# The maxima of a unit are carried by three copies of 16 rows instead of one of 48

## The reference, cut to what matters

```
x = x + 0.5 * ffn(layernorm(x))     # ffn: x and weight rounded to an MXFP4-like grid, in blocks of 32
x = x + attn(layernorm(x))          # 16 heads of 8 features, rotary positions, full softmax over 512 keys
x = x + 0.5 * ffn(layernorm(x))

scores = einsum('bhqd,bhkd->bhqk', q, k) / sqrt(8)
out    = einsum('bhqk,bhkd->bhqd', softmax(scores), v)
```

## Time and profile before

| | |
|---|---|
| median of three runs | 591.27 us |
| profiled execution | 590.53 us |
| its span, first to last instruction | 588.5 us |
| TensorE matmul busy | 487.7 us (83%) |
| VectorE busy | 438.6 us (75%) |
| ScalarE busy | 398.7 us (68%) |
| GpSimd busy | 230.9 us (39%) |
| mean granted TensorE clock | 0.947 |

### The profile page before, as it was taken

One profiled execution on the slowest core, in us unless ns is written; L12 is line 12 of the kernel. 1 busy time (PEld: TensorE's weight loads), 2 busy tenths in 40 slices (PEclk: granted clock), 3 DMA queues, 4 the chain that ended last, 5 costly groups with the idle time before them and its releaser, 6 DMA issues.

```text
span 588.5 us, 10108 instructions
## 1 busy us (share of the span) xinstructions
PE 487.7 (83%) x2662; PEld 171.2 (29%) x2662; DVE 438.6 (75%) x1020; ACT 398.7 (68%) x766; POOL 230.9 (39%) x350
## 2 busy tenths in 40 slices
PE   1261879899899998999889888999899997998861
PEld 0121223332233333333223233333233322322211
DVE  6346979785989689967968597867996686889215
ACT  4816158686868787778748685778777774778740
POOL 4401173326544455446432544346442713012300
PEclk9996599999999999999979999999999997999995
DMA  3305304500350027001600034001600161000000
GB/s 83 94 9 138 67 11 109 100 2 11 99 109 20 3 57 159 8 17 46 161 14 20 11 99 109 15 5 51 161 6 19 33 155 31 20 1 2 19 1 18
DMA packets 22590, 30.81 MB, mean 52 GB/s; under 512 B 4998, under 2 KB 20236, under 8 KB 20236
## 3 DMA queue, kind: packets, MB, share of 16 engines
q1 hardware_dynamic: 20908, 29.87, 21.0%
q10 hardware_dynamic: 1632, 0.39, 0.3%
HBM read 21.47 MB, written 8.39 MB: 51 GB/s over the span
## 4 chain that ended last, share of the span: by engine, by line
PE 52%; issue 11%; DVE 10%; DMA 9%; POOL 9%; ACT 5%; SPq 2%; POOLq 1%; DVEq 0%; ACTq 0%
PE ot L1104 15%; PE sc L1091 13%; PE st L1080 11%; DMA feat_q<-maxrows 8%; DVE negmax L878 4%; POOL qkpre L457 3%; PE misc L1027 2%; PE misc L1069 2%; ACT probs L632 2%; PE misc L1044 2%; PE misc L1052 1%; ACT feat_k L522 1%; DVE stats_f L746 1%; DMA feat_k<-parts_k 1%; PE misc L1061 1%
## 5 line engine op out<-in xcount | busy, mean ns | idle before, releaser
L878 DVE TENSOR_REDUCE negmax<-sc 128x1 f32<-128x512 f32 x512 | 333.0, 682 | 88.7 <-PE sc L1091 88.2
L632 ACT ACTIVATE probs<-st 128x512 f32<-128x512 f32 x512 | 272.4, 599 | 89.0 <-PE st L1080 87.9
L1091 PE MATMUL sc<-feat_k,feat_q 96*128 96x512 bf16 x512 | 190.4, 397 | 10.2 <-DVE negmax L878 9.1
L1080 PE MATMUL st<-feat_q,feat_k 99*128 99x512 bf16 x512 | 157.1, 384 | 16.9 <-DMA feat_q<-maxrows 10.6
L1104 PE MATMUL ot<-probs,vfeat 128*32 128x512 f32 x1024 | 139.6, 618 | 1.0 <-ACT probs L632 1.0
L1091 PEld LDWEIGHTS sc<-feat_k,feat_q 96*128 96x128 bf16 x512 | 49.9, 98 | 167.3 <-DVE negmax L878 117.0
L1080 PEld LDWEIGHTS st<-feat_q,feat_k 99*128 99x128 bf16 x512 | 49.6, 99 | 87.6 <-ACT probs L632 43.8
L457 POOL TENSOR_TENSOR qkpre<-qkpre,ropeT 128x512 f32<-128x512 f32 x28 | 35.6, 1271 | 45.7 <-ACT qkpre L581 45.7
L442 POOL TENSOR_SCALAR maxparts<-negmax 128x16 bf16<-128x16 f32 x32 | 8.2, 257 | 90.6 <-DVE negmax L878 90.6
L1044 PE MATMUL misc<-xnT,wqkT 128*128 128x512 f32 x56 | 30.8, 633 | 2.7 <-DVE onorm L895 2.0
L481 POOL TENSOR_TENSOR xres<-xres,onorm 128x128 f32 (+1 forms) x31 | 14.1, 453 | 46.9 <-DVE onorm L895 46.9
(11 more groups left out here) (132 smaller groups left out, 471.6 us busy)
## 6 DMA issues: line engine op xcount, KB each, us to landing
feat_q<-parts_q SPq DMA_DIRECT2D x48, 192.0 KB
feat_k<-parts_k SPq DMA_DIRECT2D x48, 192.0 KB
parts_q<-qkparts_q SPq DMA_DIRECT2D x24, 128.0 KB, 2.3
parts_k<-qkparts_k SPq DMA_DIRECT2D x24, 128.0 KB, 2.3
xres<-in_L_attn_x_dram SPq DMA_DIRECT2D x8, 256.0 KB, 4.8
out_dram<-xres SPq DMA_DIRECT2D x8, 256.0 KB, 2.3
feat_q<-maxrows ACTq DMA_DIRECT2D x32, 12.0 KB
wload<-in_L_ffn_weight_dram SPq DMA_DIRECT2D x1, 64.0 KB, 2.4
```

The source lines that it names most:

```text
L632: nc.scalar.activation(probs[:, s % US, j * S:(j + 1) * S], st[:, bank(2 * s + j), :], ACT.Exp, scale=SCALE).then_inc(exp_done, 1)
L878: nc.vector.tensor_reduce(negmax[:, g, j:j + 1], sc[:, bank(16 * g + j), :], AX.X, ALU.max, negate=True).then_inc(sc_maxed, 1)
L1080: nc.tensor.matmul(st[:, bank(2 * s + j), :], feat["k"][par][0:MROWS, h, kb * P:(kb + 1) * P], feat["q"][par][0:MROWS, h, :], start=True, ...
L1091: nc.tensor.matmul(sc[:, bank(16 * g + j), :], feat["q"][par][0:SROWS, h, t * P:(t + 1) * P], feat["k"][par][0:SROWS, h, :], start=True, s ...
```

## The change

`load_max_rows` issues three DMAs, one for each part, in place of one. Each carries the 16 rows of a part from 16 partitions of `maxrows` to one partition of `feat_q`. The bytes and their places are the same. Each of the three adds 16 to the semaphore, so the two waits on it count in steps of 48 (`ROWS`).

```diff
+        ROWS = PARTS * 16
...
                 if after(2 * b + g // 2):
-                    act.wait_ge(max_loaded[g % 2], 16 * (2 * b + g // 2))
+                    act.wait_ge(max_loaded[g % 2], ROWS * (2 * b + g // 2))
...
                 act.wait_ge(max_rows, G * b + g + 1)
-                act.dma_start(feat["q"][par][SROWS:SROWS + PARTS, UH * g:UH * (g + 1), :]
-                              .rearrange("a h (t q) -> a (h t) q", q=P), maxrows[:, g % 2, :]).then_inc(max_loaded[g % 2], 16)
+                n = UH * T
+                for a in range(PARTS):
+                    act.dma_start(feat["q"][par][SROWS + a:SROWS + a + 1, UH * g:UH * (g + 1), :]
+                                  .rearrange("o h (t q) -> o (h t) q", q=P),
+                                  maxrows[n * a:n * (a + 1), g % 2, :]).then_inc(max_loaded[g % 2], 16)
...
                 if s % US == 0 and j == 0:
-                    pe.wait_ge(max_loaded[g % 2], 16 * (2 * b + g // 2) + 16)
+                    pe.wait_ge(max_loaded[g % 2], ROWS * (2 * b + g // 2) + ROWS)
```

## The result

The changed kernel takes 607.52 us (median of four runs, 602.08 to 617.5) beside 590.87 us: the ratio is 1.027, with an interval of 1.019 to 1.034. It is slower, by 16.7 us of the medians. The forecast was 601 us, 10.4 us more than the kernel before, with a range of 585 to 613 us. The sign and the range hold. The forecast's own narrower range, 594 to 605 us, does not, and "the same within 2%" had been given the larger chance (0.54 against 0.36 for slower). That the time lies inside the wide range is in part luck: one term was far too small, and another came out at nothing.

The account below looks back on a forecast made before the run. TensorE, busy 487.7 of 588.5 us, was taken as the bound. Landings 7.9, spread -1.2, ScalarE's issues 1.0 and clock 2.7 gave 10.4 us on 590.53 us: 601 us, range 585 to 613 us.

Parts of the forecast that it names:

- Landing late behind the loads: Units of g = 2: the third copy stands behind loads SyncE issued meanwhile; 7.9 us, less 1.2 us for the spread.
- the seven crowded units: Units g = 2, one per batch from first to seventh, whose copies are issued while SyncE loads the next batch's features.
- The term of 7.9 - 1.2 us: Crowded g = 2 units: 7.9 us for later third copies, less 0.3 us off four landings for rows spread over more engines.
- the stall is absorbed by the wait: Units of g = 2: exponentials come 1 us late, but TensorE then waits less for the maxima, which land later still.
- No packet before all earlier loads.: Queue q10: none of a copy's packets moves before the rows of every load issued before it have started; 5.7 us in line.
- a quiet unit: One of 25 units whose copy of the maxima had 4 us or more to spare; a later landing costs nothing there.
- The first rival: Copies of the maxima: 16-row parts spread wide are served at once; 576 us, some 570 or partly 583; chance 0.15.
- ScalarE's issues: ScalarE's queue, all 32 units: three issues of 0.6 us each, 1.05 us more per unit; price 1.0 us together.
- What is queued behind them is the arithmetic of step 4: ScalarE's queue behind the three issues: the two exponentials of step 4 are what a longer issue delays.
- hidden: Step 4, one unit: with 1.05 us more issue, exponentials end at 243.4 us, just before the next can start at 243.45 us.
- The last rival: Step 4 of every unit: issues cost 0.75 us each, exponentials come 1.5 us later; 612 or 605 us; chance 0.25.
- The clock: TensorE after waits beyond 2.2 us: part of the time at 1.2 GHz instead of 2.4; one more slowdown counted, 2.7 us.

Follow-up runs that it names:

- The pair with the loads held back: SyncE's second six feature loads wait until the g = 2 maxima land: one copy of 48 rows 576.0 us, three copies of 16 rows 595.4 us.

## Why the prediction came out inside its range, and which steps were wrong

**Landing late behind the loads.** The landings moved as forecast; the waits did not. The table takes the seven crowded units in order of time. The landing is the last packet on q10, counted from the first transposed product of the unit before; "later" is the changed kernel less the kernel before. The wait is that of the first matmul that needs the maxima, and the clock is the granted one over the 5 us from there, each time before and after. All are read from the two traces (0.52 in the fourth is the 0.54 of the earlier trace rows, whose window starts 0.13 us earlier).

| | later, forecast | later, measured | wait, us | clock |
|---|---|---|---|---|
| 1 | 2.4 | 1.6 | 1.55, 2.67 | 1.00, 0.51 |
| 2 | 1.2 | 0.7 | 1.21, 1.75 | 1.00, 0.66 |
| 3 | 2.4 | 2.1 | 0, 0.79 | 1.00, 1.00 |
| 4 | 0 | 0.0 | 2.23, 0.86 | 0.52, 1.00 |
| 5 | 0 | -0.5 | 2.46, 1.29 | 0.66, 1.00 |
| 6 | 2.4 | 3.1 | 0, 1.38 | 1.00, 1.00 |
| 7 | 0 | 0.0 | 3.14, 1.69 | 0.50, 1.00 |

In the four units where I put two loads or one ahead of the last copy, the landings come 7.5 us later in all, against 7.2 in the sum (2.4 + 1.2 + 2.4 + 2.4 less 1.2 for the spread). But the waits grow by only 3.8 us there, and in the other three they shrink by 4.0 us: TensorE meets every landing later, because ScalarE's stall falls in the same unit. The term of 7.9 - 1.2 us ends as -0.2 us of wait. I did write that the stall is absorbed by the wait; then the wait has to be reckoned from TensorE's later arrival, and I had added it in full. In the chain all seven copies now stand, where five did. Two of these rows:

```profile
104.30 8.21 DMA feat_q<-maxrows
...
301.57 7.86 DMA feat_q<-maxrows
```

These are counted from a later issue of the three: the group at 300.04 us began 1.5 us before.

**"No packet before all earlier loads."** This did not hold for all packets of the new copies. Around the copies at 300.04 us, the trace has no packet on q10 from 299.9 to 301.5 us, then 24 from 301.6 to 303.2, none until 306, and 71 of the other 72 from 306 to 308.5. Eleven loads had been issued ahead, and the twelfth followed at 300.58 us. The first packet moved 1.6 us after the issue, about as in a quiet unit, the last 8.7 us after it. It is 24 early packets in each of the seven units. The maxima are complete only with the last packet, and that one came with the end of the loads. The first rival (the spread pays) saw this sign right and drew the wrong end from it. The copies have 96 packets a unit (3072 on q10 in all), which is 48 rows and 48 more, against 3 more before.

By the Trainium skill, page "DMA: Bandwidth & Descriptors", section "Why a DMA increments its semaphore by 16 and not by 1", 16 rows on both sides are spread over 16 engines; 16 further packets for each copy agree with it, as the 3 of before did. Counted in the same way, a load of 24 rows uses 12 DMA engines, for the twelve loads have 432 packets on q1, 12 each beyond their rows. That leaves four engines free, and four engines with two packets for each of three copies are 24 packets, as many as moved early. That it was these four is worked out from the counts, not seen. The 72 packets on the other twelve engines came late, so the turns between queues of its section "Queues, rings and completion order" do not show here: the kernel as a whole behaves as if the copy stood in line.

**ScalarE's issues.** The duration was right (0.6 us each), the price was wrong: 1.0 us in all, measured 2.27 us a slot at full clock and 19.5 us over the kernel. The step that failed is the sentence "What is queued behind them is the arithmetic of step 4". Behind the issues stand first the copies and normalisations of step 3, and one of them frees the bank `misc` that TensorE wants next. I worked one unit in four and carried its "hidden" over to the others. The unit of the earlier trace rows, where normalisation stands between the exponentials, had been in view, and its delay was put down as covered by the landing; that cover does not exist where the landing is early, and where it is late the two only overlap. The last rival comes closest, and its sign did come: the wait for L636 is up by 20.5 us, where more than 5 would prove it. It had the late exponentials and the size of the whole (605 to 612 us), but not the copy out of `misc`, and it wanted 0.75 us an issue; 0.6 was enough.

**The clock.** Counted as one more slowdown, 2.7 us, in the first unit. The table has it there (0.51 behind a wait of 2.67 us) and one more in the second, but the three of before, in the fourth, fifth and seventh, are gone, since their waits shrank: two in place of three. The first and the fourth:

```profile
112.55:117.55 5.00, 5.00 (x24) 1.76 (x24) 1.38 (x2) 1.08 (x2) 0.94 (x4) 0.51 0.00 0
...
309.56:314.56 5.00, 5.00 (x37) 2.13 (x41) 4.13 (x9) 2.60 (x6) 1.81 (x6) 1.00 0.01 3
```

**The sum.** 7.9 - 1.2 + 1.0 + 2.7 = 10.4 us was forecast. In the two profiles (588.5 and 600.9 us) the difference is 12.4 us, and the matmuls' waits grow by about as much: 7.2 us for the exponentials, 5.9 us for `copy_qk` and 1.6 us for the copy of the values, less 0.2 us for the maxima and about 1 us for VectorE. So nearly all of the change is ScalarE's stall, where 1.0 us had been put; the landings gave nothing, and the clock gave a little back. The pair with the loads held back differs by more, 16.4 us between the profiles and 19.5 between the medians, against 12.4 and 16.7 here. The 3 to 4 us between are of the size of the waits and of the clock that shrank in the fourth, fifth and seventh unit; they were not measured apart.

## What to carry to other kernels

A DMA issue takes its engine's instruction stream, so its price is not its duration but how long a run of issues lasts against the work in hand: in this kernel three in a row cost 19.5 us, the same three with other work between them nothing. Before calling a delay on a side engine hidden, list for every stage, not for one, what stands next in its queue and who waits for each, buffers to be freed included. And where a small transfer is late, look at what was issued ahead of it: moving six large loads behind it gained 3.7% (interval 2.6 to 4.8; 2.4% against the lowest runs of the kernel before), while no way of issuing the small one gained anything with the loads where they were.

## What the runs showed of the hardware beyond that

- An issue of 48 rows that go to three partitions takes ScalarE 747 ns, one of 16 rows 510 to 608 ns: a third of the rows saves only a fifth to a third of the issue. The shorter figure is that of issues that stand apart (median 511 ns); in a row the second and third take longer, 0.61 and 0.67 us behind a first of 0.53 (the kernel with the loads held back and three copies, at 277.08 us).
- The issue of the same 48 rows took 795 to 803 ns in the kernels where further issues follow, 747 ns where none do; why is open. In those kernels `maxrows` is also larger (128 partitions).
- A copy issued by SyncE behind its own twelve loads took 8.5 to 9.1 us from issue to landing, one issued by ScalarE amid them 8.4 to 9.9 us before the change. A queue of its own does not by itself carry a small copy past the loads, and the same queue is no better: there the issue came later, and TensorE's waits for it were 34.2 us against 17.5.
